# Cross-attention over 32 batches in fp32 pairs: the prologue gets an order table of its own, and the weights are split straight from their staged copies

## The chip, the cores and the metric

The kernel runs on one core of a Trainium2 chip. The metric is the device time of one execution in microseconds (us), median of several runs. The kernel before was timed three times: 3234.83 us in the median, 3230.63 us the lowest, 3236.19 us the highest.

## What is computed

x and ctx_1024 are both (32, 512, 512) fp32. Each is normalised over its last axis; the gains and shifts of the two norms, the four 512x512 weights and the output bias are inputs. 16 heads of 32 dimensions attend over 512 keys.

```python
qn = layer_norm(q, q_norm_g, q_norm_b)
kvn = layer_norm(kv, kv_norm_g, kv_norm_b)
Q = (qn @ Wq)...; K = (kvn @ Wk)...; V = (kvn @ Wv)...
scores = jnp.einsum('bhqd,bhkd->bhqk', Q, K) / jnp.sqrt(jnp.float32(D_HEAD))
attn = jax.nn.softmax(scores, axis=-1)
ctx = jnp.einsum('bhqk,bhkd->bhqd', attn, V)
out = q + jax.nn.gelu(ctx @ Wo + bo, approximate=False)
```

## The kernel before

**Numbers as pairs.** A product that must be exact to fp32 is made of three fast products. Each operand is split into a high part (fp32r) and a low part, the rest that the high part leaves out; high x high, high x low and low x high are summed in PSUM. That holds for the transposed inputs (`xt`), the weights (`w_hl`), Q and K. ScalarE (ACT) usually writes the high part, VectorE (DVE) the low part.

**Units.** A batch is worked in four steps; step s handles the unit of four heads with that number. For a unit, `q` and `k` are its projections (12 matmuls each, six parts of two). `s` are 16 score tiles from which only row maxima are taken (DVE, `maxes`), `m` turns the maxima, `mh`, `ml` and `mx` put them as rows into `q_stack`, `st` are the 16 transposed score tiles whose exponential ACT takes, `pv` is attention times V. `v` are the value projections, `z` the sums of rows, `o` the output projection, `x` the transposes of the next batch's input tiles (tiles 0 to 3 of x, 4 to 7 of the context). `ln`, `la`, `lv` are a tile's statistics, their aggregate and two one-column operations on DVE; POOL makes the inverse deviation, ACT then normalises (`norm`).

**Stacks.** The three products of a score are one matmul over 96 rows: `restack` sends the high part of Q (twice) and the low part (once) by DMA into rows of `q_stack`, and K likewise with high, low, high into `k_stack`. The other 32 rows hold the maxima and, in `k_stack`, a head mask (`heads_of_stack`).

**Order.** ORDER is a table with one string per engine and step; every engine works its own list in order, and semaphores hold it at a wait. Work runs ahead: in step s of batch b, `q` and `k` belong to the unit two steps on, `s` to the next unit, and `x` to the next batch. So batch -1 is a prologue: in its steps 2 and 3 the tiles of batch 0 are normalised and transposed, and its first two units projected. Before, the prologue uses the same table, sorted: in step 2 `head_rank` puts tiles first, then the rest, then `k`; in step 3 `head_rank_of_scores` puts `q` and `k` ahead.

**What only the prologue does** stands in functions `prepare`, called at fixed places. The weights land in `probs` (`L391`), which is free at that time. The gain of the norm is multiplied into the weights. For Wq POOL multiplies into a scratch tile and reorders the columns from head-major to dimension-major (`L471`); for Wk ACT does three chunks (`L549`) and POOL one (`L476`). ACT then writes the high part (`L537`) and DVE the low (`L653`), both without a stride. Wv and Wo need no reordering (`L539`, `L657`, `L655`). The shift of the norm gives biases: `bias_row_chunk` (`L800`, one-row products with Wq and Wk), `bias_row_out` on DVE (`L662`), `bias_column` (`L809`), the bias of the values (`L827`, 16 matmuls of one column), and the output bias (`L835`, `L837`, here called bo). The gen banks are three and taken in turn: the transposes of tile 1 wait for the low part of tile 0 (`L694`), tile 4 for 1, tile 5 for 2, tile 6 for 3, and tile 7 for 5. The first `q` waits for the low part of tile 7.

## Time and profile before

| what | value |
|---|---|
| median of three runs | 3234.83 us (3230.63 to 3236.19) |
| the profiled execution, its own time | 3231.49 us |
| its span, first to last instruction | 3229.7 us |
| PE, DVE, ACT, POOL busy | 99%, 70%, 71%, 72% |
| mean granted TensorE clock | 0.997 |
| first `s` matmul (L896) of the prologue | 51.64 us from the start |
| first `st` matmul (L888) | 68.71 us from the start |

Times in the views below are microseconds from the start of the span. PE is TensorE. The profile counts a busy time for each engine; the granted clock is the share of full speed that TensorE's throttle allowed. The sum of the prediction is made against the profiled execution's own time, 3231.49 us, which is 3.34 us below the median.

### The profile page before, as it was taken

What the parts mean: (1) busy time and instruction counts of PE and PEld (TensorE: products, weight loads), DVE (VectorE), ACT (ScalarE), POOL (GpSimd) and SP (SyncE); (2) the same over time, 40 slices, a digit from 0 to 9 for tenths busy, and PEclk for the clock granted to TensorE, in tenths of its full rate; (3) what the DMA queues carried; (4) which work ended last, traced back from release to release, by engine and by line L of the source; (5) the groups of instructions that cost most, each with busy time, mean ns of one, the idle gap of its engine ahead of it and who ended that gap; (6) DMA issues with size and microseconds to landing.
All of it is one profiled execution on the core that took longest, in us unless ns stands there. A gap on an engine that the chain in (4) does not pass through costs nothing.

```text
span 3229.7 us, 50112 instructions
## 1 busy us (share of the span) xinstructions
PE 3196.3 (99%) x16611; PEld 2148.0 (67%) x16611; DVE 2274.2 (70%) x4769; ACT 2306.6 (71%) x3985; POOL 2318.6 (72%) x1544
## 2 busy tenths in 40 slices
PE   8999999999999999999999999999999999999998
PEld 5566666666666666666666666666666666666664
DVE  6677677677677776776776777766767767777664
ACT  4677767777767777677777677776777776777765
POOL 2677677777777777777777777777777777777775
PEclk9999999999999999999999999999999999999999
DMA  4445445345444354453454444544534544544442
GB/s 147 101 104 129 115 119 133 95 115 137 115 115 120 104 130 115 120 133 95 115 136 116 115 119 105 130 115 121 131 95 115 138 115 114 121 105 128 115 102 79
DMA packets 193010, 376.85 MB, mean 117 GB/s; under 512 B 22625, under 2 KB 22641, under 8 KB 188658
## 3 DMA queue, kind: packets, MB, share of 16 engines
q1 hardware_dynamic: 192288, 372.86, 45.2%
q8 instruction: 134, 2.20, 0.3%
q14 instruction: 122, 1.00, 0.1%
q10 hardware_dynamic: 466, 0.80, 0.1%
HBM read 138.42 MB, written 33.82 MB: 53 GB/s over the span
## 4 chain that ended last, share of the span: by engine, by line
PE 98%; DVE 1%; ACT 1%; issue 0%; DMA 0%; ACTq 0%; POOL 0%
PE gen L868 43%; PE score L896 15%; PE score L888 15%; PE ctx L916 15%; PE gen L859 4%; PE gen L956 3%; PE gen L978 1%; DVE maxes L718 1%; PE score L800 0%; ACT probs L575 0%; PE gen L849 0%; ACT q_stack L629 0%; PE score L849 0%; ACT tok L596 0%; PE score L827 0%
## 5 line engine op out<-in xcount | busy, mean ns | idle before, releaser
L487 POOL TENSOR_TENSOR probs<-probs 128x1024 f32<-128x1024 f32 x762 | 1806.5, 2405 | 430.1 <-PE ctx L916 426.2
L718 DVE TENSOR_REDUCE maxes<-score 128x1 f32<-128x512 f32 x2048 | 1304.0, 681 | 267.8 <-PE score L896 256.7
L575 ACT ACTIVATE probs<-score 128x512 f32<-128x512 f32 x2048 | 1083.5, 606 | 229.7 <-PE score L888 219.9
L896 PE MATMUL score<-k_stack,q_stack 128*128 128x512 f32 x2048 | 728.7, 404 | 0.8 <-DVE maxes L718 0.2
L888 PE MATMUL score<-q_stack,k_stack 128*128 128x512 f32 x2048 | 713.9, 401 | 6.4 <-ACT q_stack L629 5.1
L896 PEld LDWEIGHTS score<-k_stack,q_stack 128*128 128x128 f32 x2048 | 380.0, 188 | 216.2 <-issue 81.1
L888 PEld LDWEIGHTS score<-q_stack,k_stack 128*128 128x128 f32 x2048 | 377.8, 188 | 185.6 <-ACT probs L575 42.4
L916 PE MATMUL ctx<-probs,v_sb 128*32 128x512 f32 x4096 | 492.4, 598 | 0.6 <-ACT probs L575 0.5
L868 PE MATMUL gen<-cT,w_k 128*128 128x512 f32 x1536 | 451.9, 399 | 0.1
L868 PE MATMUL gen<-xT,w_q 128*128 128x512 f32 x1536 | 444.0, 395 | 0.0
L868 PE MATMUL gen<-w_v,cT 128*128 128x512 f32 x1536 | 443.8, 390 | 0.0
L868 PE MATMUL gen<-w_o,ctx_hl 128*128 128x512 f32 x1488 | 401.5, 394 | 0.0
L503 POOL TENSOR_TENSOR rstd<-var_eps,minus_half 128x1 f32<-128x1 f32 x256 | 142.1, 555 | 322.5 <-DVE neg_mean L749 322.5
L696 DVE SCALAR_TENSOR_TENSOR k_nat<-gen,bias_k,k_nat 128x512 fp32r<-128x512 f32 x128 | 95.8, 749 | 357.9 <-ACT k_nat L620 357.9
L629 ACT ACTIVATE q_stack<-max_hl,chunk_mask 32x512 fp32r<-32x512 f32 x512 | 326.3, 706 | 29.7 <-DVE max_hl L783 28.2
L868 PEld LDWEIGHTS gen<-cT,w_k 128*128 128x128 f32 x1536 | 283.4, 191 | 80.1 <-DVE q_nat L696 27.0
L868 PEld LDWEIGHTS gen<-w_v,cT 128*128 128x128 f32 x1536 | 288.8, 188 | 62.6 <-issue 0.8
L868 PEld LDWEIGHTS gen<-xT,w_q 128*128 128x128 f32 x1536 | 288.7, 190 | 59.0
L868 PEld LDWEIGHTS gen<-w_o,ctx_hl 128*128 128x128 f32 x1488 | 274.9, 188 | 56.7
L916 PEld LDWEIGHTS ctx<-probs,v_sb 128*32 128x32 f32 x4096 | 109.3, 109 | 230.6 <-issue 206.8
L514 POOL TENSOR_TENSOR ctx_hl<-ctx_n,ctx_hl 128x512 fp32r<-128x512 f32 x128 | 164.9, 1288 | 99.8 <-ACT ctx_hl L581 99.7
L586 ACT ACTIVATE v_sb<-gen 128x512 f32<-128x512 f32 x128 | 76.1, 594 | 220.7 <-PE gen L868 220.7
(89 smaller groups left out, 2720.9 us busy)
## 6 DMA issues: line engine op xcount, KB each, us to landing
k_stack<-k_nat SPq DMA_DIRECT2D x384, 256.0 KB, 4.2
q_stack<-q_nat SPq DMA_DIRECT2D x381, 256.0 KB, 5.1
tok<-in_x SPq DMA_DIRECT2D x132, 256.0 KB, 6.0
tok<-in_ctx SPq DMA_DIRECT2D x128, 256.0 KB, 6.3
q_stack<-zero_rows SPq DMA_DIRECT2D x128, 256.0 KB, 3.3
res<-in_x SPq DMA_DIRECT2D x124, 256.0 KB, 2.6
out<-res SPq DMA_DIRECT2D x124, 256.0 KB, 2.5
probs<-in_L_xattn_Wq SPq DMA_DIRECT2D x1, 1024.0 KB, 8.5
```

Source lines behind the costliest of these rows:

```text
L487: pool.tensor_tensor(probs[:, c + 1, heads], probs[:, c + 1, heads], probs[:, c, heads], ALU.add).then_inc(pool_added, 1)
L503: pool.tensor_tensor(rstd[:, n:n + 1], var_eps[:, n:n + 1], minus_half[:], ALU.pow).then_inc(ln_rstd, 1)
L514: pool.tensor_tensor(ctx_hl[:, 1, up], ctx_n[:], raw(ctx_hl[:, 0, up]), ALU.subtract).then_inc(ctx_split, 1)
L575: act.activation(probs[:, n, part, :], score_at(s, "st", i)[:], ACT.Exp, scale=SCALE).then_inc(exp_done, 1)
L629: act.activation(q_stack[SROW:P, u1 % 2, :, P * n:P * (n + 1)], raw(max_hl[SROW:P, :]).unsqueeze(1).to_broadcast([SHIFTS, HU, P]), ACT.Ide ...
L718: dve.tensor_reduce(maxes[:, u1 % 2, SROW + i:SROW + i + 1], score_at(s, "s", i)[:], AX_X, ALU.max, negate=True).then_inc(max_done, 1)
L859: mm = pe.matmul(bank[DH * j:DH * (j + 1), :], ones[:, 0:DH], probs[:, c, j, :], start=(i == 0), stop=(i == len(chunks) - 1))
L868: mm = pe.matmul(bank[:, :], stationary(hs, c), moving(hm, c), start=(i == 0), stop=(i == len(TERMS) * NC - 1))
L888: pe.matmul(score_bank(pe, b, s, "st", i)[:, :], k_stack[:, s % 2, part, P * n:P * (n + 1)], q_stack[:, s % 2, part, :], start=True, stop= ...
L896: pe.matmul(score_bank(pe, b, s, "s", i)[:, :], q_stack[:, u1 % 2, n, P * part:P * (part + 1)], k_stack[:, u1 % 2, n, :], start=True, stop ...
L916: mm = pe.matmul(ctx_ps[DH * j:DH * (j + 1), :], v_sb[:, c, lo:lo + DH], probs[:, c, j, :], start=(c == 0), stop=(c == NC - 1))
L956: mm = pe.matmul(bank[:, P * c:P * (c + 1)], tok[:, n, P * c:P * (c + 1)], ident[:], start=True, stop=True, is_transpose=True)
```

## The change

The prologue gets a table HEAD of its own (one string per engine for each of the four steps), and the `prepare` functions and their sorting are gone; each piece of work is a token at its place in HEAD. Batches 0 and later keep ORDER. Two lines of HEAD, and the edits that carry the rest:

```diff
+HEAD = {
...
+        "ln la lv ln la lv cols ln la lv masks ln la lv x*4 ln la lv lw ln la lv lw ln la lv lw ln la lv lw "
+        "rowout x*4 rowout colout lw*4 colout bvout q k",
...
+    "sp": ("load*4 w load*4 w*3 zs", "", "rz rq rk", "rk rq rz"),
...
@@ sync
+                        if kind in ("rq", "rk") and known(b) and (b, s) == (-1, 2):
+                            sp.wait_ge(stack_used, 1)
+                            sp.wait_ge(q_hi if kind == "rq" else k_hi, 1)
+                            if kind == "rq":
+                                restack(sp, u2, q_nat, q_stack, ((0, 0), (1, 0)), q_stacked)
+                                sp.wait_ge(free["q"], 1)
+                                restack(sp, u2, q_nat, q_stack, ((2, 1),), q_stacked)
+                            else:
+                                restack(sp, u2, k_nat, k_stack, ((0, 0), (2, 0)), k_stacked)
+                                sp.wait_ge(free["k"], 1)
+                                restack(sp, u2, k_nat, k_stack, ((1, 1),), k_stacked)
...
@@ gpsimd
-                    for c in range(NC):
-                        pool.tensor_scalar(by_dim("q", scaled("q", c)), by_head("q", probs[:, 0, c, :]),
-                                           norm_cols[:, 0, c:c + 1], None, ALU.mult).then_inc(q_scaled, 1)
...
+            def heads_of_stack(slot):
+                pool.wait_ge(mask_made, 2 + slot)
+                pool.wait_ge(ln_shift, 2 * NC)
+                pool.tensor_copy(k_stack[SROW:P, slot, :, :],
+                                 head_mask[SROW:P, :].unsqueeze(2).to_broadcast([SHIFTS, HU, D])).then_inc(mask_made, 1)
...
@@ scalar
+            def high_weights(n, c):
...
+                act.activation(by_dim(w_hl[name][:, 0, c, :], name), by_head(probs[:, n, c, :], name), ACT.Identity,
+                               scale=1.0 if gain is None else norm_cols[:, gain, c:c + 1]).then_inc(w_hi, 1)
...
-                                restack(act, u2, q_nat, q_stack, ((0, 0), (1, 0)), q_stacked)
...
@@ vector
-                    if name in "qk":
-                        dve.tensor_tensor(dst, scaled(name, c), high, ALU.subtract).then_inc(w_ready, 1)
...
+                else:
+                    for u in range(NU):
+                        cols = slice(P * u, P * (u + 1))
+                        low = dve.scalar_tensor_tensor(out=dst[:, cols].rearrange("p (d j) -> p j d", j=HU),
+                                                       in0=probs[:, n, c, cols].rearrange("p (j d) -> p j d", j=HU),
+                                                       scalar=norm_cols[:, gain, c:c + 1],
+                                                       in1=high[:, cols].rearrange("p (d j) -> p j d", j=HU),
+                                                       op0=ALU.mult, op1=ALU.subtract)
+                    low.then_inc(w_ready, 1)
...
@@ tensor
-            pe.wait_ge(consts, 8)
+            pe.wait_ge(consts, 6)
...
-                if kind == "v" and b + s // (NU - 1) == 0:
-                    pe.wait_ge(w_ready, 12)
...
+                            if known(b) and (b, s) == (0, 0) and i in (0, 12):
+                                pe.wait_ge(w_ready, 12 if i == 0 else 16)
```

So the scaled scratch copies are gone: ACT multiplies, reorders and writes the high part of Wq and Wk in one instruction per chunk of 128 rows, with a write stride of 16 bytes. DVE makes the low part of a chunk in four instructions (one per unit, 128x4x32), which read the high part and write the low part with that stride. POOL does no weights; it makes the two head masks instead of DVE. On SP's queue Wq goes out before the context tiles and the zeros after all weights. The first unit's high parts of Q and K go to the stacks before their low parts are made, from SP's queue and no longer (for Q) from ACT's.

On DVE, where the statistics of the context tiles and the low parts of Wq stand. Before (from the low part of the x tiles on; L694 is the low part of a transposed tile, L653 of a weight chunk, L662 a bias row):

```order
L694 TENSOR_TENSOR xT<-gen,xT 128x4x128 x2
L742 MEMSET spare 128x1
L743 BN_AGGR moments<-stats 128x2
L748 TENSOR_SCALAR var_eps<-moments 128x1
L749 TENSOR_SCALAR neg_mean<-moments 128x1
```

and now, for tile 4 and the first two chunks (L675 is the low part of the x tiles):

```order
L675 TENSOR_TENSOR xT<-gen,xT 128x4x128 x4
L730 BN_STATS stats<-tok 128x6
L735 MEMSET spare 128x1
L736 BN_AGGR moments<-stats 128x2
L741 TENSOR_SCALAR var_eps<-moments 128x1
L742 TENSOR_SCALAR neg_mean<-moments 128x1
L652 SCALAR_TENSOR_TENSOR w_q<-probs,norm_cols,w_q 128x4x32 x4
L730 BN_STATS stats<-tok 128x6
L735 MEMSET spare 128x1
L736 BN_AGGR moments<-stats 128x2
L741 TENSOR_SCALAR var_eps<-moments 128x1
L742 TENSOR_SCALAR neg_mean<-moments 128x1
L652 SCALAR_TENSOR_TENSOR w_q<-probs,norm_cols,w_q 128x4x32 x4
```

All statistics stood ahead of the low parts of tiles 1 to 3; those of the context tiles now stand behind them, each followed by a chunk of Wq.

On TensorE, from the last transposes (L956, 128x128) to the first value projections. Before:

```order
L956 MATMUL gen<-ident,tok 128x128 x4
L800 MATMUL score<-probs,norm_cols 1x512 x5
L809 MATMUL score<-ones,res 128x1 x4
L868 MATMUL gen<-xT,w_q 128x512 x12
L809 MATMUL score<-ones,res 128x1 x4
L868 MATMUL gen<-cT,w_k 128x512 x12
L827 MATMUL score<-norm_cols,probs 128x1 x16
...
L868 MATMUL gen<-xT,w_q 128x512 x8
L835 MATMUL ctx<-probs,bias_v 128x512 x4
L837 MATMUL ctx<-bias_all,ones 128x512
L868 MATMUL gen<-w_v,cT 128x512 x4
L896 MATMUL score<-k_stack,q_stack 128x512
```

and now:

```order
L950 MATMUL gen<-ident,tok 128x128 x4
L796 MATMUL score<-probs,norm_cols 1x512
L805 MATMUL score<-ones,res 128x1 x4
L849 MATMUL gen<-xT,w_q 128x512 x12
L805 MATMUL score<-ones,res 128x1 x4
L813 MATMUL score<-norm_cols,probs 128x1 x16
L849 MATMUL gen<-cT,w_k 128x512 x24
L849 MATMUL gen<-xT,w_q 128x512 x12
L849 MATMUL gen<-w_v,cT 128x512 x2
L886 MATMUL score<-k_stack,q_stack 128x512
```

Four of the bias rows moved ahead of the last transposes, the bias of the values moved ahead of `k`, and bo is gone from this place. It stands behind `m`:

```order
L886 MATMUL score<-k_stack,q_stack 128x512 x2
L968 MATMUL gen<-ident,maxes 128x128
L822 MATMUL ctx<-probs,bias_v 128x512 x4
L824 MATMUL ctx<-bias_all,ones 128x512
L849 MATMUL gen<-xT,w_q 128x512 x6
```

## Rows read from the trace of the kernel before

**Rows 1.** The page's head, and a stretch of 100 us (columns: PE, PEld, DVE, ACT, POOL, clock)

```profile
span 3229.7 us, 50112 instructions
...
1666.00:1766.00 100.00, 99.98 (x524) 67.74 (x523) 70.91 (x149) 73.23 (x127) 74.00 (x50) 1.00 0.47 120
```

**Rows 2.** The chain that ended last, up to the first transposes (start, us, what)

```profile
5.64 1.19 DVE stats L737 x2
...
8.49 0.56 POOL rstd L503
...
9.34 2.35 ACT tok L596 x3
```

**Rows 3.** Timeline of PE (start us, us, line, what, idle before and releaser)

```profile
10.21 1.12 PE L956 MATMUL gen<-ident,tok 128*128 128x128 f32 x4 [4.78 <-ACT tok L596]
...
22.64 0.66 PE L956 MATMUL gen<-ident,tok 128*128 128x128 f32 x4
...
51.64 0.39 PE L896 MATMUL score<-k_stack,q_stack 128*128 128x512 f32 x1
...
62.61 0.30 PE L978 MATMUL gen<-ident,maxes 128*128 128x128 f32 x1 [2.18 <-DVE maxes L777]
...
68.71 0.62 PE L888 MATMUL score<-q_stack,k_stack 128*128 128x512 f32 x2
```

**Rows 4.** The chain again, from the last transposes to the first scores

```profile
23.30 4.38 PE score L800 x10
27.68 0.98 PE score L809 x8
28.66 2.94 PE gen L868 x12
...
35.52 3.46 PE score L827 x32
38.98 7.21 PE gen L868 x24
46.19 3.43 PE ctx L835 x8
49.62 1.05 PE ctx L837 x2
```

**Rows 5.** Stretches of 1 us with their granted clock (sixth column, after POOL)

```profile
41.00:42.00 1.00, 1.00 (x4) 0.81 (x3) 1.00 (x3) 0.66 (x2) 0.00 (x0) 0.50 1.02 219
...
65.00:66.00 1.00, 1.00 (x4) 0.72 (x3) 0.00 (x0) 1.00 (x3) 0.00 (x0) 0.50 0.00 0
```

**Rows 6.** Groups by shape, first 75 us (busy us, mean ns | idle before)

```profile
L549 ACT ACTIVATE tok<-probs,norm_cols 128x512 f32<-128x512 f32 x3 | 3.2, 1192 | 0.0
L657 DVE SCALAR_TENSOR_TENSOR w_v<-probs,norm_cols,w_v 128x512 fp32r<-128x512 f32 x4 | 2.7, 744 | 0.0
L539 ACT ACTIVATE w_v<-probs,norm_cols 128x512 fp32r<-128x512 f32 x4 | 2.6, 712 | 0.0
L662 DVE COPY res<-score 1x512 f32<-1x512 f32 x2 | 2.2, 1122 | 0.0
L783 DVE SCALAR_TENSOR_TENSOR max_hl<-gen,low_row,max_cut 32x128 fp32r<-32x128 f32 x1 | 0.4, 360 | 0.9 <-ACT max_cut L625 0.9
```

**Rows 7.** POOL's two reordering lines, and DVE's maxima in the timeline

```profile
L471 POOL TENSOR_SCALAR v_sb<-probs,norm_cols x4: 2073/2104/2143, 17.8 to 23.7; 128x512 f32<-128x512 f32 x4
L476 POOL TENSOR_SCALAR tok<-probs,norm_cols x1: 4363/4363/4363, 25.6 to 25.6; 128x512 f32<-128x512 f32 x1
...
53.20 9.06 DVE L718 TENSOR_REDUCE maxes<-score 128x1 f32<-128x512 f32 x15 [0.44 <-PE score L896]
```

**Rows 8.** DMA issues, us from issue to landing (first tile; stack parts; staged weights)

```profile
tok<-in_x SPq DMA_DIRECT2D x1, 256.0 KB, 2.7
...
k_stack<-k_nat SPq DMA_DIRECT2D x6, 256.0 KB, 3.6
probs<-in_L_xattn_Wq SPq DMA_DIRECT2D x1, 1024.0 KB, 8.5
```

More of the change, by code:

```diff
@@ L87, with items @@
 }
[L90 to L92 removed]
+HEAD = {
+    "pe": (
+        "", "",
+        "x*4 row*4 x row x row x row x row col q*6 col bv k*6",
+        "k*6 q*6 v s v s*2 v s v s v s*2 v s v s v s v s*2 v s v s v s*2 m bo",
+    ),
+    "act": (
+        "", "",
+        "norm*2 x norm x norm x*2 hw*4 norm*2 x norm x norm x*2 hw*4 q hw*4 k",
+        "hw*4 k q v*2 mh mx*4",
+    ),
+    "dve": (
+        "", "",
+        "ln la lv ln la lv cols ln la lv masks ln la lv x*4 ln la lv lw ln la lv lw ln la lv lw ln la lv lw "
+        "rowout x*4 rowout colout lw*4 colout bvout q k",
+        "lw*4 k s*2 q s*14 md ml lw*4",
+    ),
+    "pool": ("", "", "ln*8 heads*2", ""),
+    "sp": ("load*4 w load*4 w*3 zs", "", "rz rq rk", "rk rq rz"),
+}
+def items(table):
+    orders = [order.split() for order in table]
     early = sum(int(t.partition("*")[2] or 1) for t in orders[NU - 1] if t.partition("*")[0] == "v")
@@ new lines, in bias_of_values, with bias_of_output @@
+                        mm = pe.matmul(score[0][:, u:u + 1], probs[:, 2, c, P * u:P * (u + 1)],
+                                       norm_cols[:, 3, c:c + 1], start=(c == 0), stop=(c == NC - 1))
+                mm.then_inc(bias_mm, 1)
+            def bias_of_output():
+                pe.wait_ge(bias_cols, 3)
+                pe.wait_ge(w_loaded["o"], 16)
+                pe.wait_ge(bo_loaded, 16)
+                for u in range(NU):
+                    pe.matmul(ctx_ps[:, :], bias_v[:, u:u + 1].to_broadcast([P, P]), probs[:, 3, u, :],
+                              start=(u == 0), stop=False)
+                pe.matmul(ctx_ps[:, :], ones[0:1, :], bias_all[0:1, :], start=False, stop=True).then_inc(bo_mm, 1)
```

262 lines of the change are left out of this document (102 added, 160 removed).

## The prediction

> **What bounds the kernel now.** I read the stretches first. In a stretch of 100 us in the middle TensorE is busy for 99.98 us, DVE and ACT for some 72 [rows 1]. From batch 1 on every microsecond is TensorE's, the change leaves those batches as they are, and so it can only move the moment at which this part begins. What the prologue gains or loses reaches the end one to one. A bound of 0.2% is 6.5 us, about what a measurement of this kernel can tell from no change: the prologue would have to become a tenth shorter.
>
> Next I read the start along the chain of waits and the timeline of TensorE. The first statistics begin at 5.6 us, the first normalising at 9.34 us, the first transposes at 10.21 us [rows 2, 3]. The last transposes end at 23.3 us, and from there to the first maxima score `s` at 51.64 us TensorE is never idle: 28.3 us of bias rows, projections, the bias of the values and bo [rows 3, 4]. Then DVE sets the pace: 16 maxima, 15 of them in 9.06 us [rows 7], before `m` at 62.61 us, 11.0 us after the first `s`. From `m` to the first `st` at 68.71 us TensorE has 6.1 us of work [rows 3]. So the time in question is the sum of three pieces, (a) up to the first `s`, (b) from there to `m`, (c) from `m` to `st`. I work out each for the changed kernel.
>
> **(a), up to the last transposes.** The first tile has landed 2.7 us after its issue at 0.7, at 3.4 us [rows 8]; DVE waited till 5.6 for the columns of the norms. Now it begins at 3.4. A statistic is 0.6 us (two in 1.19 [rows 2]). The aggregate and the two one-column operations now stand right behind it, each waiting for the one before. I estimate 0.5 us for them, so 1.1 us for a tile's group; between 0.8 (almost nothing but issue) and 1.3. POOL's two operations take 0.85 us (8.49 to 9.34) and a normalising 0.78 (three in 2.35 [rows 2]). The first transposes start at about 6.5 us, 3.7 us sooner than before. That is the gain, and most of it is lost at once: tile 1's transposes use tile 0's bank and wait for its low part, which DVE now does only after all four groups, two masks and the columns, at 8.9 us. Tile 1 starts at 9.5; three rounds of 1.12 [rows 3] and half a microsecond of waiting for tile 3's norm give 13.3, then ACT's copy (0.6) and DVE's low part (0.6): 14.5 us.
>
> Now DVE alternates: a context tile's group, a chunk of Wq's low part, four times. **The price of a chunk** is the largest unknown. The same instruction costs 744 ns for 128x512 and 360 ns for 32x128 [rows 6], so 1.0 ns per element of a partition, and four of them take 2.7 us, or 0.66 us from start to start; a piece of 128 elements is then 0.28 us. It also writes with a stride of 16 bytes. ACT's strided write of 512 elements is 1192 ns against 712 ns for the straight one, 480 ns more; DVE's strided copy of one row takes 1122 ns [rows 6]. A quarter of 480 makes the piece 0.40 us. No row shows a strided read; at nothing it stays 0.40, at the price of the write it is 0.52. Ends: 0.28 and 0.52, taken 0.40, since the write stride is shown twice. A chunk is 1.6 us.
> The Trainium skill (SBUF — State Buffer, the note on 16-byte cachelines) says that every access which crosses into a new line of 16 bytes pays. The two rows on writes agree with it; read for the strided input too it would give 0.52, and x7 below would come 1.9 us later.
>
> Four rounds of 1.1 + 1.6 lead from 14.5 to 25.3; the bias row's copy (1.1 [rows 6]) to 26.4; the low parts of tiles 4 and 5 to 27.6, and only then may tile 7 be transposed (it uses tile 5's bank), ending at 28.2. Before it was 23.3: **4.9 us later**. ACT (four strided chunks from 13.9 on, 1.1 to 1.2 each [rows 6], then the norms) has done its part by about 25.
>
> **(a), from there to the first `s`.** What TensorE still has to do is less, since bias rows moved ahead into its waits and bo moved behind: one row of Wk 0.88 (five in 4.38), column 0.98, `q` 2.94, column 0.98, bias of the values 3.46, `k` 2.94, then 24 matmuls at 12 in 2.94, 5.88, and two of `v` 0.49 [rows 4]. Sum 18.6 us against 28.3. Before, the 24 took 7.21, as the clock stood at 0.50 in 41 to 42 us: 1.3 us lost. The clock also stood at 0.50 at 65 us, after 2.2 us without work before 62.61 [rows 3, 5]. TensorE will be idle some 3 us before tile 7, and the one-column matmuls that came before the first fall are still there, so I take two falls, 1.3 to 1.5 each: 2.8. First `s` at 28.2 + 18.6 + 2.8 = 49.5, **2.1 us sooner**; with one fall 3.5, with none 4.9.
>
> What hides there. Scaling on POOL and the scratch copies go; they ran beside TensorE's rows, so this is worth nothing by itself. DVE's 16 pieces for Wk (6.4 us) start near 31 and end by 38; `k` wants them at about 41. ACT no longer issues Q's three DMAs. The high parts of K are sent 0.75 us sooner: the last part of K is issued some 2 us after `k` and lands 3.6 us later [rows 8], so 5.6 us after `k`, or 7 if the queue takes a good third longer, and TensorE has 6.4 us and the lost clock to do first. Hidden, with at most 0.6 us to pay; if TensorE stays at full clock, this is late next. Wq goes out at about 2.6 us, ahead of the context tiles; even at its old 8.5 us [rows 8] it is there at 11.1, wanted at 13.3, and DVE wants tile 4 at 14.5. The zeros wait behind 4 MB of weights and land before 30. The wait for zeros holds the Q parts behind it on SP; they are ready at 35.
>
> **(b).** DVE gets the second unit's low part of Q between its maxima (0.66), less a short wait that was there: +0.3 us.
>
> **(c).** bo, 3.43 + 1.05 = 4.48 us [rows 4], stands behind `m`, where TensorE never waited: **+4.5 us**. The idle time before `m` isn't used for it. Wo's low parts lie beside it on DVE, 2.5 us, at no cost.
>
> **Sum.** -2.1 + 0.3 + 4.5 = +2.7 us. 3231.49 + 2.7 = 3234.2 for the profiled execution, and as the median stands 3.34 above that, **3237.5 us**. The front gains, the middle gains, bo is only carried over: no measurable change.
>
> **Rivals.**
> *Cheap pieces.* The strides cost DVE nothing (0.28 a piece), a group takes 0.8, and only the fall behind `m` comes. x7 3.1 us sooner, clock 2.8, and the last K part then 0.5 us late: 2.7 - 5.4 = -2.7, so 3232.1 us. For it: no row has DVE itself writing SBUF with a stride from SBUF operands. Against it: both strided rows.
> *The other side: DVE becomes the bound.* A piece costs as much as a whole instruction, 0.66 and the stride 0.12, so 0.78 us. x7 comes 16 x 0.38 = 6.1 us later, and Wk's pieces (12.5 us from 36.5 on) end at 49.0 against 48.3 when `k` wants them: 0.7 more. +9.5, 3244.3 us. It decides above 0.64 us a piece, as that brings 16 x 0.24 = 3.8 us to the 2.7. Against it: 360 ns for a small piece.
> *POOL's head masks late.* 32x2048 on POOL has no row. At L471's 2104 ns for 512 elements each takes 8.4 us; both end near 41.5, hidden. But L476, the same work, took 4363 ns while DVE made low parts from two SBUF inputs [rows 7]: 17.4 us each, till 59.5, and the first `s` waits 10 us: +12.7, 3247.5 us. It decides above 12.5 us each.
> The Trainium skill (GPSIMD Engine Reference, Key points) says that POOL shares its SBUF interfaces with DVE and contends with DVE instructions that have two SBUF inputs. The pair of rows agrees, and DVE's pieces for Wk are such instructions, which is this rival.
>
> **Numbers.** My forecast (two falls or one, pieces of 0.40 to 0.52, +0 to +6) has a chance of 0.64; cheap pieces 0.19; DVE as the bound 0.08; POOL 0.05; 0.04 is for a start that gains more than I see. Faster by over 0.2% is that 0.04 and, as single runs lay from 3230.63 to 3236.19 us, nearly half of the cheap case: 0.12. Slower is POOL, most of the DVE case, and the edge of the forecast: 0.14. Same is the rest, 0.74. The range goes from the cheap case, less 3 us for the scatter of runs, 3229, to the DVE case, 3245.
>
> **What would show it.** Right: first transposes near 6.5 us; tile 7's end near 28 us behind a gap of about 3 us put down to DVE's low part; first `s` near 49.5, `m` 11.3 us later, `st` some 10.6 us after `m`, with bo right behind `m`; pieces (128x4x32 on DVE) of 0.4 us from start to start; clock 0.50 after tile 7. Wrong: `s` waiting for masks or K parts; the first `st` before 62 us or after 75; or a middle of the trace in which TensorE isn't full any more.

## The result, and the profile after

| | before | changed |
|---|---|---|
| median, 18 runs each | 3232.76 us (3230.47 to 3236.19) | 3237.81 us (3234.66 to 3241.00) |
| ratio, with its 95% interval | | 1.0015 (1.0009 to 1.0021) |
| the profiled execution's own time, its span | 3231.49, 3229.7 us | 3239.64, 3237.8 us |
| PE, DVE, ACT, POOL busy | 99%, 70%, 71%, 72% | 99%, 70%, 71%, 71% |
| mean granted TensorE clock | 0.997 | 0.995 |
| first `s` | 51.64 us | 53.30 us |
| first `m` | 62.61 us | 65.24 us |
| first `st` | 68.71 us | 74.44 us |

The changed kernel is 5.0 us slower, a difference that the interval tells from zero, but within 0.2%. The forecast (3237.5 us, no measurable change) holds for the time and for the size, under 0.2%. It took 6.5 us as about what a measurement can tell from nothing; eighteen runs of each kernel tell 2 us. It was made from a median of three runs; eighteen put the kernel before 2.1 us lower. So the forecast difference was +2.7 us and the measured one +5.0, and that second number is what has to be explained.

TensorE's timeline in the changed kernel, from the first transposes to the first `st` (start us, busy us, engine, line, operation, output<-inputs, count, and the idle time ahead with what ended it; L950 transposes, L796 bias rows, L813 bias of the values, L822 and L824 bo):

```profile
6.37 1.12 PE L950 MATMUL gen<-ident,tok 128*128 128x128 f32 x4 [0.94 <-ACT tok L584]
...
26.21 0.86 PE L950 MATMUL gen<-ident,tok 128*128 128x128 f32 x4 [2.37 <-DVE cT L675]
27.00 1.86 PE L796 MATMUL score<-probs,norm_cols 128*1 128x512 f32 x2
...
30.59 5.49 PE L849 MATMUL gen<-xT,w_q 128*128 128x512 f32 x12
...
37.33 4.43 PE L813 MATMUL score<-norm_cols,probs 128*128 128x1 f32 x32
41.62 8.26 PE L849 MATMUL gen<-cT,w_k 128*128 128x512 f32 x24
...
53.30 0.47 PE L886 MATMUL score<-k_stack,q_stack 128*128 128x512 f32 x1 [0.25 <-issue]
...
65.24 0.30 PE L968 MATMUL gen<-ident,maxes 128*128 128x128 f32 x1 [2.18 <-DVE maxes L770]
65.37 3.66 PE L822 MATMUL ctx<-probs,bias_v 128*128 128x512 f32 x8
68.96 1.12 PE L824 MATMUL ctx<-bias_all,ones 1*128 1x512 f32 x2
...
74.44 0.62 PE L875 MATMUL score<-q_stack,k_stack 128*128 128x512 f32 x2
```

Set beside [rows 3, 4]: the start is 3.8 us sooner (6.37 against 10.21). The last transposes end at 27.0 instead of 23.3 us. The gap of 2.37 us ahead of them is put down to DVE's low part, as the prediction had it. The same 12 matmuls of `q` take 5.49 us where they took 2.94: the clock stood at its lower level. bo starts 0.13 us behind `m` and pushes `st` back.

The clock in the same stretch (window, its length, then busy time of PE, PEld, DVE, ACT and POOL with counts, the granted clock, the DMA share and GB/s):

```profile
23.00:26.00 3.00, 0.84 (x2) 0.00 (x0) 3.00 (x6) 1.30 (x2) 2.72 (x4) 1.00 0.19 63
26.00:29.00 3.00, 2.79 (x7) 0.76 (x8) 1.54 (x4) 1.89 (x3) 1.78 (x1) 0.59 0.00 0
29.00:33.00 4.00, 4.00 (x14) 3.52 (x15) 3.27 (x9) 2.69 (x3) 0.00 (x0) 0.50 0.00 0
...
40.00:44.00 4.00, 4.00 (x16) 3.52 (x16) 0.83 (x2) 0.00 (x0) 0.00 (x0) 0.52 0.14 44
44.00:47.00 3.00, 3.00 (x9) 2.32 (x8) 0.00 (x0) 0.00 (x0) 0.00 (x0) 0.50 0.21 72
47.00:53.00 6.00, 6.00 (x27) 4.64 (x25) 3.40 (x5) 2.77 (x5) 0.00 (x0) 1.00 0.54 131
```

A value of 0.50 is 1.2 GHz, 1.00 is 2.4 GHz; numbers between are windows that hold a switch. TensorE was busy for 0.84 us of the three ahead of 26. From 26.5 on (0.59 in 26 to 29) the clock stayed at the lower level for 10.2 us, to 36.8, while TensorE had work all the time. It stood there again from 40.2 to 47.0, 6.8 us, from within the 32 one-column matmuls on. Before, there was one fall in this stretch, of 3.4 us (0.57 in 40 to 44).

DVE's timeline of the changed kernel: one tile's group and one chunk of Wq, and further down what stands around the first maximum:

```profile
13.96 0.68 DVE L730 BATCH_NORM_STATS2 stats<-tok 128x6 f32<-128x512 f32 x1
...
15.03 1.53 DVE L652 SCALAR_TENSOR_TENSOR w_q<-probs,norm_cols,w_q 128x128 fp32r<-128x128 f32 x4
16.46 0.69 DVE L730 BATCH_NORM_STATS2 stats<-tok 128x6 f32<-128x512 f32 x1
...
53.91 0.75 DVE L677 SCALAR_TENSOR_TENSOR k_nat<-gen,bias_k,k_nat 128x512 fp32r<-128x512 f32 x1 [2.60 <-ACT k_nat L603]
54.57 1.28 DVE L711 TENSOR_REDUCE maxes<-score 128x1 f32<-128x512 f32 x2
```

A group takes 1.07 us (13.96 to 15.03) and a chunk 1.43 (15.03 to 16.46), 0.36 us a piece from start to start. The last two rows show a wait that the prediction didn't have: `s` began at 53.30, yet the first maximum only at 54.57, behind the low part of the second unit's K. That one waits for ACT, whose row says why:

```profile
53.18 0.69 ACT L603 ACTIVATE k_nat<-gen,bias_k 128x512 fp32r<-128x512 f32 x1 [3.29 <-DMA k_stack<-k_nat]
```

ACT may write the second unit's K only when the transfers have read the first unit's. Their last issue lies on the chain of waits (start us, length us, what):

```profile
49.12 3.98 DMA k_stack<-k_nat
```

The first unit's `k`, half of the 24 matmuls, ended at 47.1 us, and 6.0 us later its last part had landed, at 53.1, just ahead of the first `s`.

The costliest rivals of the prediction, in the groups of instructions up to 75 us (busy us, mean ns of one | idle before):

```profile
L652 DVE SCALAR_TENSOR_TENSOR w_k<-probs,norm_cols,w_k 128x128 fp32r<-128x128 f32 x16 | 5.8, 453 | 0.0
...
L543 ACT ACTIVATE w_q<-probs,norm_cols 128x512 fp32r<-128x512 f32 x4 | 4.1, 1191 | 0.0
...
L486 POOL CAST k_stack<-head_mask 32x2048 fp32r<-32x2048 f32 x2 | 3.8, 1906 | 0.2
```

POOL's masks took 1.9 us each, not 8.4 or 17.4, and `k` didn't wait for DVE's pieces.

**Where the 5.7 us up to `st` come from.** First `s` +1.66, from `s` to `m` 11.94 against 10.97 (+0.97), from `m` to `st` 9.20 against 6.10 (+3.10). Some 300 us later the distance is still 5.3 us: the `m` that stands at 381.88 us before stands at 387.22. By the last `m` it has grown. TensorE before, and in the changed kernel:

```profile
3193.75 0.33 PE L978 MATMUL gen<-ident,maxes 128*128 128x128 f32 x1
...
3201.62 0.33 PE L968 MATMUL gen<-ident,maxes 128*128 128x128 f32 x1
```

That is 7.9 us of the 8.1 by which the spans differ. The 2.5 us more came in the middle, with the clock at 1.00 and TensorE full in both (from 460 to 3170 us it waited 0.7 us in all before, and 0.2 in the changed kernel). The same work took 0.09% longer there. In e8's profile, which has the changed middle too, the distance grows likewise, from 1.4 to 3.6 us. No run tells whether the change or the execution does that. Near the end this execution also had a longer fall (0.56 over 3205 to 3212 us, against 0.57 over 3197 to 3201 before), which adds 0.3 us.

**The clock over all runs.** Every run has its mean granted clock on record. The six of the eighteen changed runs with 0.995 are the six slowest (3239.53 to 3241.00 us); the other twelve, with 0.996 or 0.997, took 3234.66 to 3238.63. So the scatter between executions goes with the clock. The mean of the eighteen is 0.9959, that of the 105 runs of the kernel before beside the experiments 0.9970. As TensorE is busy for 99% of the time, 0.0011 of 3237 us, some 3.7 us, is an estimate of what the clock has in the 5.0.

### The profile page after: what moved, and what is told of

Same layout as the page of the kernel before. It is cut to its first block, busy times and chain, and to the rows that moved or that the text cites. A ratio compares the mean times of both kernels' runs of the same rounds, so it can differ in the third digit from the quotient of the medians.

```text
span 3237.8 us, 50129 instructions
## 1 busy us (share of the span) xinstructions
PE 3204.3 (99%) x16611; PEld 2150.6 (66%) x16611; DVE 2279.8 (70%) x4791; ACT 2307.4 (71%) x3982; POOL 2311.3 (71%) x1541
## 4 chain that ended last, share of the span: by engine, by line
PE 97%; DVE 1%; ACT 1%; DMA 0%; issue 0%; POOL 0%; SPq 0%; POOLq 0%; ACTq 0%; DVEq 0%
PE gen L849 42%; PE score L886 15%; PE score L875 15%; PE ctx L908 15%; PE gen L840 4%; PE gen L950 3%; PE gen L968 1%; DVE maxes L711 0%; ACT probs L563 0%; DMA k_stack<-k_nat 0%; POOL probs L497 0%; DVE w_q L652 0%; DVE stats L730 0%; PE gen L830 0%; ACT q_stack L614 0%
## 5 line engine op out<-in xcount | busy, mean ns | idle before, releaser
L614 ACT ACTIVATE q_stack<-max_hl,chunk_mask 32x512 fp32r<-32x512 f32 x512 | 326.3, 706 | 29.8 <-DVE max_hl L776 28.2
L608 ACT ACTIVATE max_cut<-gen,cut_sign 32x128 fp32r<-32x128 f32 x128 | 46.0, 359 | 258.3 <-PE gen L968 258.3
```

The lines of the kernel that those rows point to most:

```text
L614: act.activation(q_stack[SROW:P, u1 % 2, :, P * n:P * (n + 1)], raw(max_hl[SROW:P, :]).unsqueeze(1).to_broadcast([SHIFTS, HU, P]), ACT.Ide ...
```

## The experiments

Each ratio is against the kernel before on the same chip; an interval is some 0.0018 wide, so differences below 3 us between two kernels are not settled. The profile's columns are single executions, and e8 shows how far two executions of one program may stand apart.

| run | first `s` | `m` | `st` | median us | ratio (95% interval) |
|---|---|---|---|---|---|
| before | 51.64 | 62.61 | 68.71 | 3232.76 | |
| changed | 53.30 | 65.24 | 74.44 | 3237.81 | 1.0015 (1.0009 to 1.0021) |
| e1, bo back ahead of `v` | 55.25 | 66.44 | 70.89 | 3236.24 | 1.0009 (1.0000 to 1.0018) |
| e2, bo ahead of `m` | 49.49 | 63.64 | 68.13 | 3232.71 | 1.0003 (0.9994 to 1.0012) |
| e3, before, bo ahead of `m` | 47.10 | 60.32 | 64.80 | 3229.08 | 0.9989 (0.9980 to 0.9998) |
| e4, waits filled | 49.06 | 60.99 | 70.20 | 3233.99 | 1.0005 (0.9997 to 1.0014) |
| e5, strides | 47.11 | 59.04 | 69.99 | 3232.76, one run | |
| e6, statistics in pairs | 51.96 | 63.89 | 74.82 | 3236.36 | 1.0016 (1.0007 to 1.0025) |
| e7, tiles first, bo as e2 | 47.79 | 61.20 | 65.70 | 3230.55 | 0.9995 (0.9987 to 1.0004) |
| e8, parts sent later | 49.19 | 61.12 | 70.36 | 3237.61 | 1.0018 (1.0009 to 1.0027) |
| e9, e2 and values among `s` | 45.05 | 62.03 | 66.55 | 3229.04 | 0.9992 (0.9984 to 1.0001) |
| e10, before, both moved | 43.00 | 59.81 | 64.32 | 3228.68 | 0.9987 (0.9978 to 0.9996) |
| e11, e7 and e9 together | 48.67 | 65.63 | 70.15 | 3232.81 | 1.0006 (0.9997 to 1.0015) |

### Where bo stands (e1, e2, e3)

e1 puts bo back to where it was, ahead of the first `v`; e2 puts it into the time in which TensorE waits for the maxima.

```diff
 TensorE's string of step 3 in HEAD, the changed kernel:
-"k*6 q*6 v s v s*2 ... s*2 m bo"
+"k*6 q*6 bo v s v s*2 ... s*2 m"      (e1)
+"k*6 q*6 v s v s*2 ... s*2 bo m"      (e2)
```

> The changed kernel with bo (the output bias, 4.5 us of TensorE) put back ahead of the value projections; nothing else differs. Theory 'carried over': the first s comes 4.5 us later (about 57.8 us against 53.3), the K parts have landed by then so that the first maximum follows in 0.45 us instead of 1.3, m to st shrinks from 9.2 to about 4.7 us if TensorE's clock stays up after m, or 6.1 if it falls there as in the kernel before. Total: between 0.8 us less and 0.8 us more than the changed kernel, so +4 to +6 us against the kernel before. Rival 'bo behind m is the loss': the kernel comes within 1 us of the kernel before, since the 4.5 us behind m would be hidden at the old place.

> The changed kernel with bo between the last s and m, where TensorE was idle for 2.2 us. Theory: the idle time is used, m comes 2.3 us later (67.5 us against 65.2) and st follows it in about 4.7 us, at 72.3 us against 74.4: 2.2 us less than the changed kernel, about +3 us against the kernel before. Rival: m's chain (maxima turned, rows written into the stack, 3.7 us) becomes what st waits for, or delaying m delays the units behind it, and the gain is under 0.5 us.

e3 does the same to the kernel before, whose statistics and weights stay as they were:

```diff
                 if (kind, b, s) == ("v", -1, 3):
                     pe.wait_ge(bias_cols, 3)
+                if (kind, b, s) == ("m", -1, 3):
...
-                        if kind in ("v", "st", "k") and (n, part) == (0, 0) and known(b):
+                        if kind in ("v", "st", "k", "m") and (n, part) == (0, 0) and known(b):
```

> The kernel before with bo between the last s and m, everything else as it was. Theory: the first s comes 4.5 us sooner (47.1 us), K's parts have landed at 43.1; the 2.2 us without work ahead of m are filled, so m comes at 60.4 against 62.6, and the fall of TensorE's clock that followed that idle time (1.4 us) goes: 2.2 to 3.6 us less than the kernel before. Rival: the first s waits for the stack parts and the gain stays under 1 us.

e1 can't be told from the changed kernel (1.0009 and 1.0015, the intervals overlap by most of their length): no gain or loss from carrying bo from one end of the scores to the other is shown, and one of 2 us or somewhat more isn't excluded. The rival, a time within 1 us of the kernel before, didn't come: e1 is 4.0 us above it on its chip. e2 stands 3.5 us below e1 in the median, on the same chip, and its ratio 1.2‰ below the changed kernel's. TensorE in e2:

```profile
59.06 3.59 PE L822 MATMUL ctx<-probs,bias_v 128*128 128x512 f32 x8
...
63.64 0.33 PE L968 MATMUL gen<-ident,maxes 128*128 128x128 f32 x1
```

There is no wait ahead of `m` now, and half of bo lies in the time that was idle. The kernel before gains as much from it. TensorE in e3:

```profile
47.10 0.39 PE L897 MATMUL score<-k_stack,q_stack 128*128 128x512 f32 x1
...
60.32 0.33 PE L979 MATMUL gen<-ident,maxes 128*128 128x128 f32 x1
...
64.80 0.61 PE L889 MATMUL score<-q_stack,k_stack 128*128 128x512 f32 x2
```

First `s` 4.5 us sooner, `s` to `m` 2.3 us longer, and `m` to `st` 4.48 instead of 6.10, since no fall of the clock followed: 3.9 us in this profile, 3.2 in the medians. (A fall doesn't follow each 2.2 us wait ahead of `m`: it did before, in e5 and e6, and didn't in the changed kernel, e1, e4 and e8.)

### The wait ahead of tile 7 and the clock (e4, e6, e8)

e4 gives TensorE 16 more matmuls in its two waits, 4 ahead of tile 6 and 12 ahead of tile 7. They write a bank that nobody reads then, and add nothing to the output.

```diff
-"x*4 row*4 x row x row x row x row col q*6 col bv k*6"
+"x*4 row*4 x row x row fill x row fill*3 x row col q*6 col bv k*6"
...
+                        if kind == "fill":
+                            for _i in range(4):
+                                pe.matmul(ctx_ps[:, :], xt["x"][:, 0, 0, 0:P], xt["x"][:, 0, 0, :], start=True, stop=True)
```

> The changed kernel with 16 more matmuls whose result nobody reads, 4 ahead of tile 6's transposes and 12 ahead of tile 7's, in the time in which TensorE waits there (0.9 and 2.4 us). Theory 'the idle time lets the clock fall': the granted clock stays at 1.00 from 26 to 36 us, q takes 2.9 us instead of 5.4, the first s comes about 4.5 us sooner (near 49 us), or limited by the last K part near the same; total 3 to 5 us less than the changed kernel. Rival 'the slow clock there comes from the thin matmuls (one row or one column wide), not from the idle time': the clock is at 0.50 after tile 7 as before and the time is the same or 0.3 us more.

```profile
23.79 3.02 PE L867 MATMUL ctx<-xT 128*128 128x512 f32 x12
26.65 0.60 PE L953 MATMUL gen<-ident,tok 128*128 128x128 f32 x4
...
29.11 3.06 PE L849 MATMUL gen<-xT,w_q 128*128 128x512 f32 x12
```

In this timeline of TensorE tile 7 ends at 27.2, as late as in the changed kernel. Yet `q` takes 3.06 us instead of 5.49, and the first `s` comes 4.2 us sooner. That alone shows little, as e2 and e8, with the wait unfilled, also have profiles in which `q` takes 3.0 us (below). The runs carry it: the ratio falls from 1.0015 to 1.0005, the single runs of the two hardly overlap (3232.02 to 3235.33 against 3234.66 to 3241.00), and the mean clock of e4's eleven runs is 0.9970 against 0.9959. Work that computes nothing made the kernel some 3 us faster. That is what the waits cost through the clock, on average and beyond their own length. A fall remains (36.0 to 42.7 us) that begins while the one-column matmuls run.

e6 tests the other half of the wait, its length. The statistics of the context tiles stand in pairs, and the four chunks of Wq behind them:

```diff
-... x*4 ln la lv lw ln la lv lw ln la lv lw ln la lv lw "
+... x*4 ln*2 la lv la lv ln*2 la lv la lv lw*4 "
```

> The changed kernel with the statistics of the four context tiles in front of all four low-part chunks of Wq on DVE instead of between them. Theory: the tiles' norms are then ready 3 to 4 us sooner, but tile 7's transposes still wait for tile 5's low part, which stands behind the chunks and the bias row, so that they come only some 0.5 us sooner; time within 1 us of the changed kernel unless the clock falls elsewhere. Rival 'the alternation on DVE is what loses the front': tile 7 ends 3 us sooner and the time falls by 3 us.

Nothing came of it, as expected: 1.0016, and tile 7 at 26.36 us. The chunks stay ahead of the low parts of tiles 4 and 5, for which tile 7 waits, and DVE's sum of work up to there is the same.

e8 leaves everything as it is in the changed kernel up to 36 us, and sends the first unit's high parts only when the low ones are ready, so that "sent ahead" is undone:

```diff
-                            sp.wait_ge(q_hi if kind == "rq" else k_hi, 1)
+                            sp.wait_ge(free["q" if kind == "rq" else "k"], 1)
```

> The changed kernel with the first unit's stack parts sent only when the low part is made (high, high, low in one go, as before), for Q and K. Theory: the last K part is issued one or two issues of 0.6 us later, the K stack lands about 0.8 us later after k, and as the first s stood right at that landing, s and the second unit's K come 0.8 us later: +0.5 to +0.8 us. Rival 'hidden anyway': no difference. The program is the same as the changed kernel's up to 36 us, so the clock in that stretch also shows how much it differs between executions of one program: if it depends on the program alone it is at 0.50 from 26.2 to 36.4 us again.

The ratio is 1.0018 against 1.0015: sending ahead is worth nothing that can be measured, and the wait before the first `s` is 0.75 us where it was 0.25. But its timeline of TensorE told more:

```profile
26.30 0.66 PE L950 MATMUL gen<-ident,tok 128*128 128x128 f32 x4 [2.36 <-DVE cT L675]
...
28.81 3.02 PE L849 MATMUL gen<-xT,w_q 128*128 128x512 f32 x12
...
49.19 0.47 PE L886 MATMUL score<-k_stack,q_stack 128*128 128x512 f32 x1 [0.75 <-issue]
```

The same program, the same wait of 2.36 us ahead of tile 7, and no fall behind it: `q` takes 3.02 us. In this execution the first `s` came 4.1 us sooner than in the changed kernel's profile, and the medians are the same. The execution itself took 3235.41 us, 2.2 below its kernel's median; the profiled one of the changed kernel took 3239.64, 1.8 above. Three more profiles have the same program up to `q` and the same wait of 2.37 us ahead of tile 7: e1 with a fall of 3.4 us behind it (27.0 to 30.4), e9 with one of 6.8 (26.8 to 33.6), e2 with none. So **whether a fall follows the wait, and how long it lasts, differs between executions** (10.2, 6.8, 3.4 us, none and none in these five), and the profile of the changed kernel shows the longest. Medians have to carry every verdict on the clock; a single profile can only show that a fall is possible and what it costs.

### What the strides cost DVE (e5)

Wq's chunks 0 and 1 and Wk's 2 and 3 keep the write stride, all of Wq is read without a stride, all of Wk with one. Where the write is straight, the reordering of the low parts is left out.

```diff
+                        far, near = "p (d j) -> p j d", "p (j d) -> p j d"
+                        to = far if (n, c // 2) in ((0, 0), (1, 1)) else near
+                        of = far if n == 1 else near
...
-                        low = dve.scalar_tensor_tensor(out=dst[:, cols].rearrange("p (d j) -> p j d", j=HU),
+                        low = dve.scalar_tensor_tensor(out=dst[:, cols].rearrange(to, j=HU),
...
-                                                       in1=high[:, cols].rearrange("p (d j) -> p j d", j=HU),
+                                                       in1=high[:, cols].rearrange(of, j=HU),
```

> The changed kernel with the strides of DVE's low-part pieces taken apart, chunk by chunk: Wq chunks 0 and 1 write with the 16-byte stride and read straight, Wq chunks 2 and 3 neither, Wk chunks 0 and 1 read the high part with the stride and write straight, Wk chunks 2 and 3 both. The reordering of the low parts is left out where they are straight. The pieces took 0.36 us from start to start with both strides (5.84 us for 16), 0.28 was expected with none and 0.40 with the write's. If the write stride costs what it cost ACT (0.12 us a piece) and the read nothing: 0.36 to 0.40, 0.28, 0.28, 0.36. If the strides cost DVE nothing and the small pieces are simply dearer than the line through 512 and 128 elements says: 0.36 in all four. If both strides cost half each: 0.32, 0.28, 0.32, 0.36.

DVE's timeline: one chunk of Wq with the write stride alone and one with none, each with the statistic that begins behind it, and the sixteen pieces of Wk, eight of them with the read stride alone and eight with both:

```profile
17.11 1.23 DVE L655 SCALAR_TENSOR_TENSOR w_q<-probs,norm_cols,w_q 128x128 fp32r<-128x128 f32 x4
18.18 0.67 DVE L733 BATCH_NORM_STATS2 stats<-tok 128x6 f32<-128x512 f32 x1
...
19.23 1.13 DVE L655 SCALAR_TENSOR_TENSOR w_q<-probs,norm_cols,w_q 128x128 fp32r<-128x128 f32 x4
20.28 0.69 DVE L733 BATCH_NORM_STATS2 stats<-tok 128x6 f32<-128x512 f32 x1
...
27.51 5.87 DVE L655 SCALAR_TENSOR_TENSOR w_k<-probs,norm_cols,w_k 128x128 fp32r<-128x128 f32 x16
```

The instructions of DVE overlap at their ends, so a chunk is read from its start to the start of what follows. Four pieces: 1.05 us straight (19.23 to 20.28), 1.07 with the write stride (17.11 to 18.18), 1.43 with both (the changed kernel). Sixteen of Wk take 5.87 us, as with both strides everywhere (5.8), so taking the write stride from half of them gained nothing. A piece is 0.26 us straight and 0.36 with both; the read stride costs it 0.09 us (a quarter of 1.43 - 1.07), the write stride under 0.01. The prediction's 0.40 us a piece was near the measured 0.36 for the wrong reason: it took the price of a write from ACT and none for the read. The Trainium skill (SBUF — State Buffer, the note on 16-byte cachelines) has every access pay that crosses into a new line. The reads here agree with it; DVE's write does not show it, while ACT's does (1191 ns against 708 for a straight chunk in the changed kernel).

### Tiles first (e7)

DVE takes a tile's low part as soon as it can, all chunks of weights stand behind the last tile, ACT and TensorE likewise, and bo stands ahead of `m` as in e2:

```diff
-"x*4 row*4 x row x row x row x row col q*6 col bv k*6"
+"x*4 row x row x row x row x row*4 col bv q*6 col k*6"
...
-"ln la lv ln la lv cols ln la lv masks ln la lv x*4 ln la lv lw ln la lv lw ln la lv lw ln la lv lw "
-"rowout x*4 rowout colout lw*4 colout bvout q k"
+"ln la lv ln la lv cols x ln la lv ln la lv x ln la lv x ln la lv x ln la lv ln la lv x*4 "
+"rowout lw*4 masks rowout colout lw*4 colout bvout q k"
```

> The changed kernel's instructions in another order: on DVE the context tiles' statistics and the low parts of tiles ahead of all low parts of Wq, on ACT the eight tiles ahead of the weights, on TensorE the four bias rows of Wk and the bias of the values behind tile 7, and bo ahead of m. Theory 'the front is lost because tile 7 stands behind the Wq chunks': tile 7 is transposed at about 20 us and the thin matmuls stand in one piece without idle time, first s near 44 to 48 us depending on the clock, st near 63 to 66 us: 1 to 3 us less than the same kernel with only bo moved (3232.7 us), near 3230. Rival: the weights become what q and k wait for, since ACT and DVE now come to them 4 us later, and the time is that of the kernel with only bo moved or more.

```profile
20.81 0.66 PE L950 MATMUL gen<-ident,tok 128*128 128x128 f32 x4
...
39.22 5.53 PE L849 MATMUL gen<-cT,w_k 128*128 128x512 f32 x16 [2.13 <-DVE w_k L652]
```

TensorE's timeline has tile 7 at 20.8 us, 5.4 sooner than in the changed kernel and 1.8 sooner than before. It came back only in part, since `k` now waits 2.13 us for DVE's chunks of Wk; e11 shows below that POOL's masks hold these chunks up. Median 3230.55 us, 0.9995: 0.8‰ below e2's ratio, a difference that isn't settled, and not to be told from the kernel before.

### The bias of the values among the scores (e9, e10, e11)

The 32 one-column matmuls stand on the path ahead of `s`. In all ten profiles in which they stand together (before, changed, e1 to e8) a fall begins while they run or within 1.5 us of their end. e9 starts from e2 and spreads them over four places among the scores, where TensorE waits for DVE anyway; the copy of their result comes behind the 13th maximum.

```diff
-"... col q*6 col bv k*6"
-"k*6 q*6 v s v s*2 v s v s v s*2 v s v s v s v s*2 v s v s v s*2 m bo"
+"... col q*6 col k*6"
+"k*6 q*6 v s bv v s*2 v s bv v s v s*2 bv v s v s v s v s*2 bv v s v s v s*2 bo m"
```

> The kernel with bo ahead of m, and besides the bias of the values (16 matmuls of one column, 3.5 us) taken out of its place ahead of k and put in four pieces among the s, into the bank that bo uses. Theory 'the thin matmuls of that bias let the clock fall over k and q': the fall that begins some 5 us after it started (40.4 us in the kernel before and in the changed one) is gone, k k q take 8.8 us, first s near 43 to 46 us. As TensorE then has 12.7 us of work among the s where DVE had set the pace with 10.4, m comes 2.3 us later after s, bo waits for the copy of the bias and no longer fills the idle time. Together between 1 us more and 2 us less than the kernel with only bo moved (3232.7 us). Rival: the fall is still there.

e10 does both moves in the kernel before (the lines that carry the matmuls and DVE's copy to their new places are left out):

```diff
-                if (kind, b, s) == ("q", -1, 3):
-                    pe.wait_ge(w_loaded["v"], 16)
+                if (kind, b, s) == ("v", -1, 3):
                     pe.wait_ge(bias_cols, 2)
...
-                if (kind, b, s) == ("v", -1, 3):
+                if (kind, b, s) == ("m", -1, 3):
                     pe.wait_ge(bias_cols, 3)
...
+                            if known(b) and (b, s) == (-1, 3) and i in (0, 3, 6, 11):
+                                bias_of_values((0, 3, 6, 11).index(i))
```

> The kernel before with both sets of thin matmuls moved: the bias of the output between the last matmul of the scores and the first of the next part (as in e3), and the bias of the values in four pieces among the scores. Theory (the 4.4 us of one-column matmuls stand on the path and a clock fall follows them): the first matmul of the scores starts at 43 to 44 us instead of 47.1 in e3, the stretch from there to the first m grows from 13.2 to about 16 us because TensorE now has work among the scores, the first st at about 63.5 us; with no clock fall at 40 us the median is 3226 to 3229 us, 0 to 3 us below e3 and 3 to 6 us below the kernel before. Rival (TensorE among the scores becomes the pace, or the clock falls somewhere else in the preparation all the same): first st at 64.8 us or later and a median of 3229 to 3231 us, no better than e3 alone.

e9 brings the changed order to 0.9992, 1.1‰ below e2, where at most 2 us were expected; that difference isn't settled either. In its profile there is one fall up to 76 us, behind the wait for tile 7 (26.8 to 33.6 us), and none at 40. e10 is the fastest of all, 0.9987 (0.9978 to 0.9996), 5.1 us below the kernel before on its chip. TensorE in e10:

```profile
43.00 0.47 PE L900 MATMUL score<-k_stack,q_stack 128*128 128x512 f32 x1 [1.57 <-DMA k_stack<-k_nat]
...
59.81 0.33 PE L984 MATMUL gen<-ident,maxes 128*128 128x128 f32 x1
...
64.32 0.62 PE L892 MATMUL score<-q_stack,k_stack 128*128 128x512 f32 x2
```

First `s` 4.1 us sooner than in e3, as expected, and the clock stays at 1.00 from 23 us to 80. But `st` comes only 0.5 us sooner. TensorE waits 1.57 us for the K stack, and from there on it has work without a gap. So its own work between the last tile and `st` has become the bound. e10 can't be told from e3 by its ratio either; both beat both kernels.

e11 asks whether the gains of e7 and e9 add up: e9's kernel with e7's strings.

> The changed kernel with the tiles first on DVE, ACT and TensorE (as in e7) and both sets of thin matmuls moved (as in e9): bo ahead of m, the bias of the values in four pieces among the scores. If what e7 and e9 each gained adds up: tile 7 is transposed at about 21 us, TensorE has some 22 us of work from there to the first score, so the first s at 43 to 44 us, m at about 60 us (TensorE the pace), the first st at 64 to 64.5 us, the median 3226 to 3228.5 us, below e9 (3229.04). If TensorE's own work from the last tile to the first st is the bound, as the run before this one suggests, it ends where that did: st at 64.3 us and 0.999 of the kernel before, and the two gains do not add up.

They don't: 1.0006, against 0.9995 and 0.9992 for either alone. TensorE:

```profile
32.12 2.11 PE L850 MATMUL gen<-cT,w_k 128*128 128x512 f32 x8
39.32 6.32 PE L850 MATMUL gen<-cT,w_k 128*128 128x512 f32 x16 [5.09 <-DVE w_k L652]
```

TensorE reaches `k` sooner by the bias of the values, and waits 5.09 us for the chunks of Wk. The clock fell in that wait (0.61 in 37 to 40 us, 0.55 in 40 to 45). The chunks on DVE:

```profile
23.83 5.80 DVE L652 SCALAR_TENSOR_TENSOR w_q<-probs,norm_cols,w_q 128x128 fp32r<-128x128 f32 x16
...
30.99 8.28 DVE L652 SCALAR_TENSOR_TENSOR w_k<-probs,norm_cols,w_k 128x128 fp32r<-128x128 f32 x16
```

Sixteen pieces took 5.80 us, and the next sixteen, the same work, 8.28. The head masks had moved behind Wq, and POOL copied them just then:

```profile
30.18 3.91 POOL L486 CAST k_stack<-head_mask 32x2048 fp32r<-32x2048 f32 x2 [10.95 <-DVE head_mask L630]
```

DVE's timeline cut off at 34.2 us shows that two pieces alone bear the loss:

```profile
30.99 3.33 DVE L652 SCALAR_TENSOR_TENSOR w_k<-probs,norm_cols,w_k 128x128 fp32r<-128x128 f32 x2
```

They took 1.32 and 2.09 us, and each ended 0.24 us after one of POOL's copies (32.31 and 34.33 against 32.07 and 34.09); the other fourteen took 0.43 each. Both began after the copy beside them. e7 has the same collision (the two took 3.32 us there). DVE lost some 2.5 us by it, half of e11's wait and more than e7's 2.13; no run has the masks at another place in this order. In the kernel before it was POOL that came second and waited, from 0.04 us behind the first of four low parts of DVE with two SBUF inputs:

```profile
25.58 2.47 DVE L653 TENSOR_TENSOR w_q<-v_sb,w_q 128x512 fp32r<-128x512 f32 x4
...
25.62 4.36 POOL L476 TENSOR_SCALAR tok<-probs,norm_cols 128x512 f32<-128x512 f32 x1
```

POOL ended at 29.98, 1.93 us after DVE's last (28.05), and 1.95 us is what the same work took it alone (L471, from start to start). In all these pairs the one that began second ended only behind the other: DVE's piece by 0.24 us, POOL's by its whole own time.

## Why the prediction was right, and where it was not

**The bound: right for the start, not quite for the middle.** The middle stayed full (PE 99%), and the shift at `st`, 5.7 us, was still 5.3 at 387 us. But "one to one" to the end didn't hold in the profiles: 7.9 us at the last `m`, and what made the 2.5 more is open.

**(a), up to tile 7: right, 1.2 us too late.** First transposes 6.37 for 6.5; group 1.07 for 1.1; piece 0.36 for 0.40; the low part of tile 3 done at 14.0 for 14.5; tile 7 ends at 27.0 for 28.2. The half microsecond at tile 3 and sixteen pieces at 0.04 make up the difference. The reason for the price of a piece was wrong (e5).

**(a), from there to `s`: the term that failed.** The work was counted right, 18.6 us. "I take two falls, 1.3 to 1.5 each: 2.8" was the step: 18.6 us of work took 26.3 (27.0 to 53.3), so 7.7 us were lost. There were two falls, at the foreseen places, but of 10.2 and 6.8 us instead of the 3.4 that the profile of before showed, and TensorE did little more than half as much in them. "2.1 us sooner" became 1.7 later. Much of that miss is this execution's: e8 ran the same start with one fall of 6.8 us and had `s` at 49.19, 0.3 us from the forecast. That closeness is luck in part, since tile 7 was 1.2 us sooner than forecast and `s` then waited 0.75. A typical execution probably lies between the two, as their times lie on either side of the median. What the first wait's fall costs on average is best read from the medians, with e4: about 3 us, where the sum had 1.4; the clocks of all runs say 3.7 for all falls together, where the sum had 1.5 more than before.

**(b): +0.3 forecast, +0.97 measured.** The sum knew the second unit's low part of Q, but not that of K, which comes late because the first unit's K is still being read (`k_nat`). e8, which sends the high parts later, had the same 11.93 us from `s` to `m`.

**(c): +4.5 forecast, +3.1 measured.** bo behind `m` costs 4.6 us (65.37 to 70.01), as said. But the stretch of before held a fall of its own at 64.0 to 67.4 us, which the changed kernel's profile doesn't have. The sum left that fall where it was. e1 agrees with the reading that bo was only carried over, within its noise, and e2 shows that the idle time ahead of `m` is its place.

**The sum:** +3.8, +0.7 and -1.4 against the three terms turn +2.7 into +5.7 in the profile, and the medians have +5.0. For the profiled execution the sum said 3234.2 us, and it took 3239.64. That the median came out within 0.3 us is luck: the median that the sum was added to lay 2.1 us too high, and the difference 2.3 us too low.

**The rivals.** Cheap pieces: no, 0.36 against its 0.28, and the fall that it left out came. DVE as the bound: not in the changed kernel; e7 and e11 show it as soon as TensorE comes sooner. K's stack, "hidden, with at most 0.6 to pay, late next": 0.25 us paid, and 1.57 in e10. POOL's masks late: 1.9 us each, dead. Its ground was misread: L476's 4363 ns was no slower rate but one wait for DVE's 2.47 us, then its own time, so it doesn't scale to 17.4 us a mask. In e11 it came out in the other direction: POOL kept its 1.95 us a mask (1.94 in the changed kernel) and DVE lost 2.5 us. The Trainium skill (GPSIMD Engine Reference, Key points) says that the two share their SBUF interfaces and contend then; e11 and the kernel before agree, and in both the one that began second paid. In the changed kernel the masks (23.91 to 27.78 us) stood almost wholly beside DVE work with an input in PSUM, and took 1.92 and 1.89 us.

**What stays open.** Why a fall lasts 3.4 us in one place and 10.2 in another, and how often it follows the wait for tile 7, can't be read from one profile for each kernel. Nor is it known why the middle took 2.5 us more. How the 5.0 us divide isn't settled: bo ahead of `m` (e2) and filled waits (e4) each won back over 3, and no run has just these two together. That the one-column matmuls bring on the fall behind them is supported by e9, e10 and e11, where they are spread and none follows, and by the ten profiles with a fall at them; but where they were spread, other things had moved too, and no run changed their width alone.

## What to carry to other kernels

A wait of TensorE costs its length and, in some executions, a stretch at half clock behind it: order the work in a prologue so that TensorE doesn't run dry, and look for work that can stand in the waits that remain (bo ahead of `m` was worth 3 to 4 us in either kernel). A new order that starts one engine sooner is worth nothing if another engine's sum of work up to the next hand-over stays the same; here the chunks between the tiles moved the last transposes 3.7 us back and spent the 3.8 us won at the start. Two moves that each gain can lose together (e11): after each one, ask again which engine the next wait belongs to, and what now stands beside what.

## What the hardware showed that was not expected

- **Falls of the clock differ between executions of one program, and in length**: 3.4 us before, 10.2 and 6.8 us in the changed kernel; behind the same wait of some 2.4 us 10.2, 6.8, 3.4 us, none and none (changed, e9, e1, e2, e8). The Trainium skill (TensorE: Matmul & The Clock Gate, Part 1: The HAM clock gate) says that the monitor behind the gate runs freely and does not start with the kernel, so that the moment of a switch varies from run to run. The traces agree in that, and differ besides in whether a fall comes at all and how long it lasts.
- **Matmuls that compute nothing sped the kernel up** by about 3 us (e4), with tile 7 no sooner.
- **Strides on DVE**: per piece of 128 elements 0.09 us for a strided second input, under 0.01 for a strided output (e5, from start to start); on ACT a strided output of 512 elements costs 480 ns.
- **POOL beside DVE with two SBUF inputs**: they took turns by whole instructions. Two DVE pieces that began during POOL's copies took 1.32 and 2.09 us instead of 0.43 (e11) and POOL lost nothing; before, POOL's 1.95 us took 4.36 behind 2.47 us of DVE's.
